# A layer norm on 32-feature slices in place of one on whole rows, inside a graph layer kernel

## What is computed

```python
m = mean(x, axis=-1); v = var(x, axis=-1)
n = maximum((x - m) / sqrt(v + 1e-5), 0.0)      # layer norm, then ReLU
h = item_feat @ W_item.T + b_item               # 10000 x 128
b = n @ W_user.T + b_user                       # 10000 x 128
return x + relu(adj @ h + b)                    # adj is 10000 x 10000
```

## Time and profile before

| What | Value |
|---|---|
| Median of 3 runs | 1114.21 us (1113.17 to 1114.88) |
| Profiled execution, its own time | 1113.8 us |
| Its span in the profile | 1112.0 us |
| TensorE busy | 1101.9 us, 99% |
| VectorE busy | 972.7 us, 87% |
| ScalarE busy | 768.1 us, 69% |
| DMA | 421.50 MB, 379 GB/s on average |

### The profile page before, as it was taken

One profiled execution on the slowest core, in us unless ns is written; L12 is line 12 of the kernel. 1 busy time (PEld: TensorE's weight loads), 2 busy tenths in 40 slices (PEclk: granted clock), 3 DMA queues, 4 the chain that ended last, 5 costly groups with the idle time before them and its releaser, 6 DMA issues.

```text
span 1112.0 us, 12241 instructions
## 1 busy us (share of the span) xinstructions
PE 1101.9 (99%) x5026; PEld 904.1 (81%) x5026; DVE 972.7 (87%) x692; ACT 768.1 (69%) x491; POOL 31.0 (3%) x62
## 2 busy tenths in 40 slices
PE   8999999999999999999999999999999999999998
PEld 7788788888888788888887888888788888888887
DVE  6999988889998888899998888999987889888887
ACT  5766766677776667776766677777766767776664
POOL 0000000001000000010000000000000000000000
PEclk9999999999999999999999999999999999999999
DMA  9999999999999999999999999999999999999994
GB/s 358 414 426 393 380 360 364 372 366 380 427 382 378 386 368 389 391 389 425 379 376 386 359 405 388 391 423 375 386 366 379 398 354 401 410 367 352 370 382 165
DMA packets 64904, 421.50 MB, mean 379 GB/s; under 512 B 7999, under 2 KB 8787, under 8 KB 25040
## 3 DMA queue, kind: packets, MB, share of 16 engines
q1 hardware_dynamic: 60128, 406.15, 93.1%
q0 software_dynamic: 4432, 14.44, 3.8%
q10 hardware_dynamic: 288, 0.13, 0.0%
HBM read 415.57 MB, written 5.12 MB: 378 GB/s over the span
## 4 chain that ended last, share of the span: by engine, by line
PE 91%; DVE 5%; DMA 1%; issue 1%; ACT 1%; SPq 0%; DVEq 0%; ACTq 0%
PE acc L578 29%; PE acc L571 29%; PE acc L572 29%; DVE lo_ring L379 4%; PE acc L544 2%; PE acc L521 1%; DMA a_ring<-in_adj_tiles 1%; ACT hi_ring L315 1%; DVE y L459 1%; PE acc L537 1%; PE acc L554 0%; DVE centred L422 0%; DVE stat L418 0%; SPq L219 0%; SPq L237 0%
## 5 line engine op out<-in xcount | busy, mean ns | idle before, releaser
L379 DVE TENSOR_TENSOR lo_ring<-a_ring,hi_ring 128x2048 fp32r<-128x2048 f32 (+1 forms) x387 | 861.5, 2239 | 120.3 <-ACT hi_ring L315 119.9
L315 ACT CAST hi_ring<-a_ring 128x2048 fp32r<-128x2048 f32 (+1 forms) x387 | 725.1, 1874 | 326.4 <-PE acc L578 321.6
L571 PE MATMUL acc<-hi_ring,h_lo 128*128 128x512 f32 (+1 forms) x1560 | 614.0, 394 | 1.2 <-ACT hi_ring L324 0.6
L578 PE MATMUL acc<-lo_ring,h_hi 128*128 128x512 f32 (+1 forms) x1560 | 603.0, 387 | 3.7 <-DVE lo_ring L379 3.7
L572 PE MATMUL acc<-hi_ring,h_hi 128*128 128x512 f32 (+1 forms) x1560 | 599.9, 385 | 0.0
L578 PEld LDWEIGHTS acc<-lo_ring,h_hi 128*128 128x128 f32 x1560 | 292.9, 188 | 68.1 <-DVE lo_ring L379 7.5
L571 PEld LDWEIGHTS acc<-hi_ring,h_lo 128*128 128x128 f32 x1560 | 293.1, 188 | 65.8 <-issue 9.1
L572 PEld LDWEIGHTS acc<-hi_ring,h_hi 128*128 128x128 f32 x1560 | 293.5, 188 | 61.9 <-issue 4.6
L521 PEld LDWEIGHTS acc<-wi,items 128*128 128x128 f32 x156 | 22.0, 196 | 2.0
L273 POOL DMA_DIRECT2D rows<-in_x_rows x20 | 10.9, 546 | 419.9 <-DVE centred L422 375.9
L521 PE MATMUL acc<-wi,items 128*128 128x128 f32 x156 | 22.2, 280 | 0.0
(11 more groups left out here) (31 smaller groups left out, 118.3 us busy)
## 6 DMA issues: line engine op xcount, KB each, us to landing
a_ring<-in_adj_tiles SPq DMA_DIRECT2D x311, 1024.0 KB, 7.1
a_ring<-in_adj_tiles SPq DMA_DIRECT2D x78, 904.0 KB, 6.6
rows<-in_x_rows POOLq DMA_DIRECT2D x19, 256.0 KB, 6.1
y<-in_x_t POOLq DMA_DIRECT2D x19, 256.0 KB, 7.1
items<-in_item_t SPq DMA_DIRECT2D x12, 384.0 KB, 7.7
out_t<-y POOLq DMA_DIRECT2D x16, 256.0 KB, 6.4
a_ring<-in_adj_tiles SPq DMA_DIRECT2D x4, 256.0 KB, 5.2
out_t<-y SPq DMA_DIRECT2D x3, 256.0 KB, 2.5
```

The costliest lines, as they stand in the source:

```text
L315: nc.scalar.copy(hi_ring[:, r, 0:group_w(g)], a_ring[:, s, 0:group_w(g)]).then_inc(hi_written, 1)
L379: nc.vector.tensor_tensor(lo_ring[:, r, 0:n], a_ring[:, s, 0:n], hi_ring[:, r, 0:n], ALU.subtract).then_inc(lo_written[s], 1)
L571: nc.tensor.matmul(acc[k][:, 0:bank_w(g, k)], h_lo[:, c, :], hi, start=(c == 0), stop=False, skip_group_check=True)
L578: last = nc.tensor.matmul(acc[k][:, 0:bank_w(g, k)], h_hi[:, c, :], lo, start=False, stop=(c == CHUNKS - 1), skip_group_check=True)
```

## The change

The layer norm keeps the users on the free axis and puts the features in four slices of 32 on the partitions: `rows` is now 128 partitions (slice, user within a block of 32) by 64 blocks by 32 features, for the whole group. A partition's reduction gives the sum over one slice only. TensorE adds the four slices and divides by 128 with one matmul per group, by a constant matrix `spread` (loaded by DMA), once for the means and once for the variances. After scaling, VectorE turns each 32x32 block in place of TensorE's transposes, and the result has features on the partitions at once. The copy out of PSUM goes too. `squares` shares its memory with `normed_t`, one unit's worth, so units take turns in it.

The steps of a group are now at these tiles: sums 14 to 17, mean product 19, centrings 22 to 25, squares 25 to 28, sums of squares 26 to 29, variance product 31, eps 34, root on ScalarE 37, root steps on VectorE 38 (once per group, on 64 columns), scaling and block transpose 39, 45, 51, 57, user products 41, 47, 53, 59. The rows of the next group are loaded by POOL after the block transpose of the same unit; those of group 0 once 6, 8, 10 and 12 roundings are done.

The diff, cut to its core:

```diff
-CENTRE_AT = 4
-SQUARE_AT = 7
-VAR_AT = 8
+SUM_AT = 14
+MEAN_AT = 19
+CENTRE_AT = 22
+SQUARE_AT = 25
+SUM_SQUARES_AT = 26
...
+            act.dma_start(spread[:, :], mean_of).then_inc(spread_loaded, 16)
             act.dma_start(wi[:, :], w_item_t).then_inc(w_item_loaded, 16)
...
             def square(g, k):
-                n = row_t(g, k)
-                act.wait_ge(centred_ready, g * UNITS + k + 1)
-                nc.scalar.activation(squares[0:n, :, :], centred[0:n, :, :], ACT.Square).then_inc(squares_ready, 1)
...
+                u, b = g * UNITS + k, blocks(g, k)
+                n = b.stop - b.start
+                act.wait_ge(centred_ready, u + 1)
+                if k > 0:
+                    act.wait_ge(squares_summed, u)
+                elif g > 0:
+                    act.wait_ge(user_done, u)
+                nc.scalar.activation(squares[:, 0:n, :], rows[:, b, :], ACT.Square).then_inc(squares_ready, 1)
...
-            def copy_turned(g, k):
-                act.wait_ge(turned_ready, g * UNITS + k + 1)
-                nc.scalar.copy(normed_t[:, 0:bank_w(g, k)], turned_of(g)[:, 0:bank_w(g, k)]).then_inc(normed_t_ready, 1)
...
+            def sum_rows(g, k):
+                b = blocks(g, k)
+                dve.wait_ge(rows_loaded[k], 16 * (g + 1))
+                nc.vector.reduce_sum(sums[:, b], rows[:, b, :], AX_X).then_inc(summed, 1)
...
             def centre(g, k):
+                b = blocks(g, k)
+                dve.wait_ge(mean_ready, g + 1)
+                nc.vector.tensor_tensor(rows[:, b, :], rows[:, b, :], means_of(g)[:, b].unsqueeze(2).broadcast_to(wide(b)),
                                         ALU.subtract).then_inc(centred_ready, 1)
...
+            def sum_squares(g, k):
+                u, b = g * UNITS + k, blocks(g, k)
+                n = b.stop - b.start
                 dve.wait_ge(squares_ready, u + 1)
+                nc.vector.reduce_sum(sums[:, b], squares[:, 0:n, :], AX_X).then_inc(squares_summed, 1)
...
             def norm(g, k):
...
+                dve.wait_ge(normed_ready, u + 1)
+                if k > 0:
+                    dve.wait_ge(user_done, u)
+                nc.vector.transpose(normed_t[:, 0:n, :], rows[:, b, :]).then_inc(normed_t_ready, 1)
...
             def warm(times):
                 for _ in range(times):
-                    nc.tensor.matmul(warm_bank[0:ROW_T, 0:ROW_T], ident[:, :], ident[:, :], start=True, stop=True, skip_group_check=True)
+                    nc.tensor.matmul(warm_bank[:, 0:P], spread[:, :], spread[:, :], start=True, stop=True, skip_group_check=True)
...
-                for t in range(ROW_TILES):
-                    last = nc.tensor.transpose(turned[:, t * n:(t + 1) * n], normed[0:n, t, :], ident[0:n, 0:n])
-                last.then_inc(turned_ready, 1)
...
+            def mean_product(g):
+                n = blocks(g, UNITS - 1).stop
+                if g > 0:
+                    pe.wait_ge(y_ready[0], g)
+                pe.wait_ge(summed, UNITS * (g + 1))
+                nc.tensor.matmul(means_of(g)[:, 0:n], spread[:, :], sums[:, 0:n], start=True, stop=True,
+                                 skip_group_check=True).then_inc(mean_ready, 1)
...
-            pe.wait_ge(ident_set, 1)
+            pe.wait_ge(spread_loaded, 16)
             warm(WARM_FIRST)
```

More of the change, by code:

```diff
@@ L74 @@
 WARM_THEN = 6
[L76 removed]
+assert 0 < LAST_BANK_W <= BANK_W <= BANK_PITCH and BANK_W % BLOCK == 0 and SLICES * BLOCK == P
 assert CHUNKS % S_SLOTS == 0 and CHUNKS % A_SLOTS == 0 and CHUNKS % TRIO == 0 and A_SLOTS % TRIO == 0
@@ L141, in graph_layer @@
         h_full_rem = sb("h_full_rem", [REM, HID])
-        ident = sb("ident", [ROW_T, ROW_T])
+        spread = sb("spread", [P, P])
         y = sb("y", [P, ACC_BANKS, BANK_W])
[L144 to L149, removed]
+        rows = sb("rows", [P, GROUP_BLOCKS, BLOCK])
+        normed_t = sb("normed_t", [P, UNIT_BLOCKS, BLOCK])
+        squares = normed_t
+        stat = sb("stat", [P, 5, GROUP_BLOCKS])
+        sums, var, std, inv, root = (stat[:, i, :] for i in range(5))
         banks = [[ctx.enter_context(nc.psum_tensor(f"acc{half}{k}", [P, 512], F32)) for k in range(ACC_BANKS)] for half in range(2)]
@@ L171, in graph_layer @@
         ones_loaded = sem("ones_loaded")
-        rows_loaded = sem("rows_loaded")
-        ident_zero = sem("ident_zero")
-        ident_set = sem("ident_set")
+        rows_loaded = [sem(f"rows_loaded{k}") for k in range(UNITS)]
+        spread_loaded = sem("spread_loaded")
         h_done = sem("h_done")
@@ L365, in _ @@
                         h_rem_round()
[L366 to L369, removed]
+                    k = unit_at(c, SQUARE_AT, 1)
+                    if k is not None:
+                        square(g, k)
+                    if c == SQRT_AT:
+                        root_of_var(g)
         @block.vector
@@ L494, in _ @@
                         empty(g - 1, 3)
-                    for at, step in ((CENTRE_AT, centre), (VAR_AT, variance), (NORM_AT, norm)):
-                        k = unit_at(c, at)
+                    if c == EPS_AT:
+                        add_eps(g)
+                    if c == ROOT_AT:
+                        root_step(g)
+                    for at, every, step in ((SUM_AT, 1, sum_rows), (CENTRE_AT, 1, centre), (SUM_SQUARES_AT, 1, sum_squares), (NORM_AT, NORM_EVERY, norm)):
+                        k = unit_at(c, at, every)
                         if k is not None:
@@ L543, in user_product @@
                 pe.wait_ge(normed_t_ready, g * UNITS + k + 1)
-                nc.tensor.matmul(acc_of(g)[k][:, 0:bank_w(g, k)], wu[:, :], normed_t[:, 0:bank_w(g, k)], start=False, stop=False,
-                                 skip_group_check=True)
+                columns = normed_t[:, :, :].rearrange("p b i -> p (b i)")[:, 0:bank_w(g, k)]
+                nc.tensor.matmul(acc_of(g)[k][:, 0:bank_w(g, k)], wu[:, :], columns, start=False, stop=False,
+                                 skip_group_check=True).then_inc(user_done, 1)
             def left_over(g):
```

152 lines of the change are left out of this document (74 added, 78 removed).

## The result

| What | Before | Changed |
|---|---|---|
| Median of 4 runs | 1114.55 us (1113.17 to 1115.49) | 1141.32 us (1140.21 to 1142.06) |
| Profiled execution, its own time | 1113.8 us | 1140.21 us |
| Its span | 1112.0 us | 1138.4 us |

The changed kernel is slower by 2.4% (ratio 1.0242, 95% interval 1.0230 to 1.0254). The forecast was 1139.0 us, made against the profiled execution's 1113.8: +25.2 us where that execution shows +26.4.

A forecast was written before the change was run, and what follows sets the result against it. TensorE's issue time was taken to bound the kernel. Transposes, products, tile 5, start and added wait summed as 1113.8 - 8.8 + 1.6 - 1.3 - 1.1 + 34.8 = 1139.0 us, range 1132 to 1146, eight in ten 1130 to 1150.

The forecast's parts named there:

- The added wait: Squares sharing one buffer at tiles 26 to 30 make ScalarE and VectorE run in turn: +34.8 us over five groups.
- Turn: One round of rounding, subtraction, sum and square at tiles 26 to 29: 5.39 us against 2.72 for a normal tile.
- The transposes: 80 transposes leave TensorE's queue, 0.44 us a unit by distance of starts: -8.8 us.
- The products: Ten 64-column products with fresh weights added on TensorE, 0.16 us each: +1.6 us (1.1 to 2.2).
- Tile 5: Centring 0 leaves tile 4, ending a TensorE delay of 0.36 us in four groups: -1.3 us.
- The start: First product slips about 2.2 us, 0.2 stays; the 1.34 us wait at 30.09 goes: net -1.1 us.
- VectorE: Moved steps: lag 0.09 us per tile, root steps about 1.3 us, block transpose 0.69 us; nothing shows on TensorE.
- the cover: Left-over products (1.14 us) before tile 40 and slack hide VectorE's work, until the block transpose exceeds about 1.22 us.
- The wait is covered: Rival: slack hides the squares' wait at tiles 26 to 30, only other terms count: 1104 us, chance 0.06.
- TensorE's pace falls in the stalls: Rival: each group's stalls halve the matmul clock, 3 us lost five times: 1154 us, chance 0.10.
- The block transpose is slow: Rival: VectorE's block transpose takes 2.2 us, exceeding the cover by 1 us a unit: 1156 us, chance 0.05.
- The transposes were dearer: Rival: TensorE's removed transposes cost 270 ns each, 12.8 us more gain: 1126 us, chance 0.03.

The follow-up runs named there:

- e1: The changed kernel with each unit's squares in their own bank of y and x loaded after the sum: 1103.47 us, ratio to before 0.9904.
- e2: The changed kernel with VectorE summing the squares ahead of its tile's subtraction, buffer and wait kept: 1104.22 us, ratio to before 0.9910.
- e4: The kernel before, with each unit's set of four transposes issued twice: 1122.07 us, ratio to before 1.0073.
- e5: e1 with warm-up matmuls reading memory set by POOL instead of spread, and wi loaded ahead of spread: 1103.97 us, ratio to before 0.9906.
- e6: e1 with the left-over products four tiles later, before tile 44 instead of 40: 1106.74 us, ratio to before 0.9932.
- e3: e1 with units 2 and 3 sharing a bank, so only square 3 waits (one turn): 1115.68 us, ratio to before 1.0011.
- e8: e3 with units 1, 2 and 3 sharing a bank, so squares 2 and 3 wait (two turns): 1130.96 us, ratio to before 1.0149.
- e7: e5 with a group's four emptyings one to a tile at tiles 1 to 4, not two and two: 1103.23 us, ratio to before 0.9900.

## Why the prediction held, step by step

- **The added wait** was the term that decided, and it came as worked out. The square's 15 waits are there, 3.2 us each (2.9 predicted). Turn: 5.39 predicted, 5.44 measured. Loss per group: 7.0, three times 7.1, 6.5 predicted; 7.55, three times 7.3, 6.7 measured against e1. Sum +34.8 against 36.3. Half of the missing 1.5 us is the turn, short by 0.05 three times in each of five groups; more than half of the rest is group 0, whose turn was guessed from group 1's and not worked out from its own casts and additions. That e2 gets rid of the loss with buffer and wait in place shows the cause is the cycle through both in-order queues.
- **The transposes:** -8.8 predicted. e4 gives 8.1 for the same number added. In e1 against before, a group's tiles (36 to 36 of the next) gain 1.8 us in groups 0 to 2, and four units at 0.44, two products at +0.225 and tile 5 at -0.46 make 1.77. By whole tiles the two prices are each a little higher: tiles 13 and 14 of group 1 last 3.08 and 2.83 us before and 2.72 each in e1, so 0.47 a unit (0.47 to 0.50 over the four), and tiles 18 and 19 last 2.86 and 2.85 us in e1, so 0.27 a product. The difference lies in the matmuls behind an inserted instruction, which start slightly further apart for the rest of their tile. In the sum of a group the two corrections cancel but for 0.1 us.
- **The products** were sized too low: 1.6 taken, 2.2 the upper bound. TensorE's timeline in group 1:

```profile
308.75 0.39 PE L609 MATMUL acc<-lo_ring,h_hi 128*128 128x512 f32 x1
308.97 0.33 PE L561 MATMUL acc<-stat,spread 128*128 128x64 f32 x2
309.11 0.47 PE L602 MATMUL acc<-hi_ring,h_lo 128*128 128x512 f32 x1
309.43 0.39 PE L603 MATMUL acc<-hi_ring,h_hi 128*128 128x512 f32 x1
```

  L609 to L603 is two matmul steps (0.455 us) and one product: 0.68 - 0.455 = 0.225 us, ten times 2.25 (2.7 by whole tiles). Half the columns did not halve the price.
- **Tile 5:** -1.3 predicted, about -2.0 measured (0.46 to 0.60 per group between tiles 4 and 8). The delay in the earlier trace rows was priced at 0.36 us by the distance to one start (four times that is 1.4, not 1.3); the next step, 0.33 us in place of 0.23 (265.79 to 266.12 before), lies on top.
- **The start:** -1.1 predicted; at tile 8 of group 0 the changed kernel is 1.5 us ahead, e1 1.95. The first product slips by 2.05 us (2.2 predicted), but only by 1.22 in e1, whose start is the same program: the six records of the first `h` products take 0.83 us there and 1.33 in the changed kernel, so the 2.05 came out near in part by luck. e5 shows that the slip is absorbed.
- **VectorE:** the lag per tile with one added instruction is 0.08 us (0.09 predicted); the block transpose has a mean of 700 ns (0.69 predicted); the root steps were 0.5 us too cheap in the sum, since 1.1 ns a column, taken from a subtraction, does not hold for a reciprocal. It changed nothing, as the left-over products had room for it; e6 shows the cover to be real.

The errors have both signs (+1.5, +0.65, -0.7, -0.4) and cancel in part. By the terms as measured, -8.8 + 2.25 - 2.0 - 1.5 + 36.3 is 26.3 us; the profiled execution shows 26.4. That this agrees to 0.1 us is luck, since two differences that no term holds nearly cancel. In group 0, between tiles 8 and 26, e1 gains 0.7 us over before and the changed kernel 0.4, where each gains 1.4 in groups 1 to 3. And the last group gains 2.6 us in e1, where groups 1 to 3 gain 1.85: a tile of it lasts 2.42 us until something is inserted between the products of the large product, and 2.47 in most tiles from there on, which is from the first transposes (tile 14) before, and only from tile 42 in e1 and in the changed kernel. Why the longer step lasts is not known.

**The rivals.** *The wait is covered* did not come, but e1 and e2 are this case built on purpose, and 1103.5 and 1104.2 stand against its 1104. *TensorE's pace falls in the stalls* came in part: the mechanism is real, at three places in the changed kernel, and wrong was only that it would be paid each time; a turn leaves TensorE idle long enough to make the slow matmuls up. In e3 and e8, where the stall is the last one, it was paid, 1.5 to 1.6 us each where two groups can be compared; the rival had put it at 3. *The block transpose is slow* fell by its own row (372.14 above, 0.71 us). The Trainium skill, VectorE: DVE Perf Modes (The three transpose paths), gives 311 ns for 128 columns of bf16. Four times that, an estimate for 512 columns, would be 1.24 us; 0.71 was measured for 512 columns of float32, so the estimate by columns is too high here. The measured 0.71 us sits well inside the cover of 1.22 us. *The transposes were dearer* fell by e4.

**What stays open.** In group 0 the changed kernel loses another 0.5 us between tiles 14 and 18 that e1 does not, where roundings wait for loads (13.7 us in 13 waits over the span, but e1 has 13.4 in 13); two traces can't tell whether this is the kernel or the loads' own spread. Nor is it known why the pace fell in three groups out of five: up to the drop, groups 1, 2 and 3 have the same standstills to 0.05 us. In e7 it fell at the start, during a wait of 1.53 us (product at 21.52 us), and in e5 the same wait (product at 22.38 us) had no drop.

## What to carry to other kernels

When two in-order engines share a buffer, write down what each waiting instruction stands behind: if the release stands behind work that needs the waiter's next step, the engines take turns, and the price is the whole turn less the normal tile, once per handover, with the slack paid out only once. The cheapest cure may be order, not memory: moving one 0.68 us instruction ahead of a 2.3 us one brought back 37 us. Price what you take from a full queue by the distance between starts, and what you add by an instruction of the same kind, not of the same size.

## What the runs showed of the hardware that was not expected

- RECIPROCAL on VectorE takes 0.17 us for 4 columns and 0.55 for 64: 6.3 ns for each further column, against 0.19 to 0.23 us for the other operations of 64 columns (the root's rows under e6).
- A float32 product of 64 columns with new weights holds TensorE's queue 0.225 us (0.27 with what follows in its tiles), as long as a fast-format matmul of 512 columns does (0.23), while a transpose of 128 columns holds it 0.10 to 0.11.
- The granted clock fell to half (0.52 in the window's row) for 3.4 us behind two standstills of 1.51 and 1.59 us with one of 0.55 between them, and also in e3 behind a single one of 1.59 us. Standstills of 1.52, 0.51 and 1.59 us in group 3, and in before a wait of 1.34 us at 30.09, had no such effect.
- After a standstill TensorE's second matmul starts 0.33 to 0.35 us behind the first and not 0.23, so even a short wait has a fixed price of its own.
